# A state-space layer and a mixture of experts on one core: the ring of scan inputs, four slots or three

## The reference, cut to what matters

```python
h = x * rsqrt(mean(x * x) + EPS) * norm_scale
xs, res = split(h @ w_in, 2)
xs = silu(causal_depthwise_conv(xs, conv_w, conv_b)); res = silu(res)
delta, B, C = split(xs @ w_xproj, [dt_rank, dt_rank + N])      # N = 16 states
delta = softplus(delta @ w_dt + b_dt)
deltaA = exp(delta[..., None] * A)                             # A = -exp(A_log)
deltaBx = (delta * xs)[..., None] * B[:, :, None, :]
ys[t] = deltaA[t] * ys[t-1] + deltaBx[t]                       # the scan over time
y = einsum('blcn,bln->blc', ys, C)
x = layernorm(x + x + ((y + xs * D) * res) @ w_out)
```

## Time and profile before

| | before |
|---|---|
| time, median of 3 runs | 2160.95 us (2160.07 to 2165.15) |
| the profiled execution, its own time | 2160.5 us |
| its span | 2158.7 us |
| busy over the span: PE, DVE, ACT, POOL | 79%, 61%, 41%, 40% |
| mean granted clock of TensorE | 0.917 |

### The profile page before, as it was taken

The page is one execution under the profiler, slowest core; times in us unless marked ns, Lnnn a source line. Parts: engine busy times, 40 slices in busy tenths (PEclk is TensorE's granted clock), DMA queues, the critical chain, the costliest instruction groups (busy, mean ns, idle before and its releaser), DMA issues.

```text
span 2158.7 us, 20606 instructions
## 1 busy us (share of the span) xinstructions
PE 1710.6 (79%) x5491; PEld 821.9 (38%) x5492; DVE 1327.1 (61%) x1984; ACT 882.4 (41%) x1598; POOL 862.5 (40%) x399
## 2 busy tenths in 40 slices
PE   7387877878778787787765999949999999999900
PEld 2121312213122131221103767626666666676600
DVE  3379989798797987979994344413333333333345
ACT  4457556574565745657442333301221212212100
POOL 0766849577595775957850222210000000000065
PEclk9699989999899898998997999979999999999955
DMA  4633425334253342533416510010110101101033
GB/s 125 144 77 92 106 55 141 80 93 103 56 141 80 93 103 56 140 79 93 102 39 220 192 39 29 30 66 25 34 33 31 34 31 33 32 31 34 25 114 122
DMA packets 105433, 169.86 MB, mean 79 GB/s; under 512 B 14624, under 2 KB 53264, under 8 KB 105248
## 3 DMA queue, kind: packets, MB, share of 16 engines
q1 hardware_dynamic: 99232, 152.44, 27.3%
q0 software_dynamic: 6144, 16.79, 2.4%
HBM read 127.76 MB, written 41.42 MB: 78 GB/s over the span
## 4 chain that ended last, share of the span: by engine, by line
PE 52%; DVE 26%; ACT 8%; issue 7%; POOL 3%; DMA 3%; SPq 1%; another core or an unknown queue 0%; DVEq 0%; ACTq 0%; POOLq 0%
DVE psH L900 17%; PE psA L1382 12%; PE psP L1399 12%; DVE X L909 6%; PE psP L1228 5%; PE psP L1307 5%; PE psH L1316 5%; PE psA L1265 5%; PE psH L1390 3%; ACT psH L746 2%; PE psP L1217 2%; POOL gat L460 1%; PE psP L1236 1%; ACT L746 1%; DMA ud_dram<-ud 1%
## 5 line engine op out<-in xcount | busy, mean ns | idle before, releaser
L407 POOL TENSOR_TENSOR X<-rep,B 128x2048 f32<-128x2048 f32 x128 | 577.0, 4522 | 246.0 <-PE psA L1265 231.9
L1265 PE MATMUL psA<-X,gsum 128*32 128x512 f32 x1024 | 466.0, 677 | 238.7 <-DVE X L909 238.6
L746 ACT ACTIVATE psH<-rep,A_q 128x512 f32<-128x512 f32 x512 | 349.9, 689 | 123.6 <-DVE X L909 114.6
L900 DVE TENSOR_TENSOR_SCAN psH<-psH,X 128x512 f32<-128x512 f32 x256 | 313.0, 1223 | 119.6 <-ACT psH L746 75.6
L900 DVE TENSOR_TENSOR_SCAN psH<-psH,carry,X 128x512 f32<-128x512 f32 x256 | 329.8, 1288 | 48.0 <-ACT psH L746 48.0
L909 DVE TENSOR_TENSOR X<-psH,C 128x512 f32<-128x512 f32 x512 | 347.3, 679 | 0.0
L460 POOL DMA_INDIRECT gat<-eo_dram,slots x64 | 62.7, 980 | 664.9 <-DVE slots L1143 644.4
L1265 PEld LDWEIGHTS psA<-X,gsum 128*32 128x32 f32 x1024 | 59.7, 113 | 618.7 <-DVE X L909 575.9
L1382 PE MATMUL psA<-ew_s,nTb 128*128 x576 | 268.1, 608 | 0.8 <-ACT nTb L821 0.8
L1399 PE MATMUL psP<-ew_s,hT 128*128 x1152 | 262.2, 381 | 2.6 <-ACT hT L827 2.6
L1399 PEld LDWEIGHTS psP<-ew_s,hT 128*128 128x128 f32 x1152 | 220.0, 191 | 63.3 <-issue 36.8
(11 more groups left out here) (172 smaller groups left out, 1597.3 us busy)
## 6 DMA issues: line engine op xcount, KB each, us to landing
rep<-ud_dram SPq DMA_DIRECT2D x128, 512.0 KB, 8.7
ud_dram<-ud SPq DMA_DIRECT2D x32, 512.0 KB, 5.0
ew_s<-in_L_ffn_ew_dram SPq DMA_DIRECT2D x16, 1024.0 KB
xb<-rows_dram SPq DMA_DIRECT2D x72, 128.0 KB, 2.0
eo_dram<-eo SPq DMA_DIRECT2D x72, 128.0 KB, 1.7
B<-bc_dram SPq DMA_DIRECT2D x128, 64.0 KB, 2.3
C<-bc_dram SPq DMA_DIRECT2D x128, 64.0 KB, 2.1
out_dram<-fin SPq DMA_DIRECT2D x8, 512.0 KB
```

The source lines that it names most:

```text
L407: nc.gpsimd.tensor_tensor(X[:, Q % NX], rep[:, g % 2, 1], B4[:, f:f + 1, :].broadcast_to([P, NR, TC]), ALU.mult).then_inc(bx_ready, 1)
L746: nc.scalar.activation(psH[:, r, :], rep[:, g % 2, 0, r, :], ACT.Exp, scale=A_q[:, c, r, f:f + 1]).then_inc(dA_ready, 1)
L900: nc.vector.tensor_tensor_scan(psH[:, r, :], psH[:, r, :], X[:, Q % NX, r, :], start, ALU.mult, ALU.add).then_inc(scan_done, 1)
L1265: ins = nc.tensor.matmul(psA[r * GJ:(r + 1) * GJ, g % 2, :], gsum[:], X[:, Q % NX, r, :], start=False, stop=(f == NF - 1), skip_group_chec ...
```

## The change

The ring `X` has three slots instead of four. Nothing else is edited; the slot of step Q is `Q % NX` in the three places that use it (L407, L900 and L909, L1265), and POOL's wait at L406 is `y_acc >= Q - NX + 1`, so that it now waits for step Q - 3 where it waited for step Q - 4. The views of `X` that the start of the program uses (`vrows`, `st1`, `mv1`, `junk1`) lie in slots 0 to 2 and stay. `X` is the last tile of stage 1, so that no other tile moves; the 8 KB per partition stay unused.

```diff
         B4 = sb("B4", [P, NF, TC])
         C4 = sb("C4", [P, NF, TC])
-        NX = 4
+        NX = 3
         X = sb("X", [P, NX, NR, TC])
         vrows = X[:, 0, 0, 0:P]
         st1 = X[:, 1, 0, 0:NSUBS * 6].rearrange("p (t s) -> p t s", s=6)
```

## The result

| | before | after |
|---|---|---|
| time, median of 5 runs each | 2161.65 us (2160.07 to 2165.15) | 2175.09 us (2170.68 to 2177.53) |
| ratio, 95% interval | | 1.0052 (1.0040 to 1.0064) |
| profiled execution: span | 2158.7 us | 2173.3 us |
| end of the last scan in it | 1142.3 us | 1156.8 us |
| from there to the end | 1016.5 us | 1016.6 us |

The change costs half a per cent, and all of it in stage 1: behind the last scan the two profiles take the same time. The ratio in the table is taken from all the runs; the quotient of the two medians alone is 1.0062. The forecast was slower, 2171.3 us or a ratio of 1.0048, in a range of 2163.5 to 2174.5. Both ratios lie in that range, which is 1.0012 to 1.0063 of the 2160.95 us that it was set against. The median in us lies 0.6 us above it, 0.7 us of which come from the kernel before, whose median is 2161.65 with two more runs.

A forecast was written before the change was run, and what follows sets the result against it. DVE was the fullest engine, waiting mostly for ACT's exponential rather than POOL. Seven tile delays summed to 10.35 us, giving 2170.9 us profiled and 2171.3 us as median (ratio 1.0048), range 2163.5 to 2174.5.

The forecast's parts named there:

- What bounds: Stage 1: DVE, the fullest engine, waits for POOL only twice, 43.9 us, at the start; POOL waits for the ring.
- The chunk behind step 12: Tile 3, POOL: step 12 waits for PE's step 9, so chunk 0 of the next tile starts 2.28 us late.
- The transfers: SP's queue, tile 3: transfers land in issue order, so late loads of rep delay chunk 1's store and ACT 2.28 us.
- Is it given back?: DVE after step 14 of tile 3: no later wait found that recovers the 2.2 us, so the whole shift stays.
- The sum: Tiles 0 to 6: DVE delays of 0.35 to 2.25 us per tile add up to 10.35 us.
- the unknown: Where TensorE's lower clock falls: 5.6 us if PE's step 9 is quick everywhere, 11.3 if slow in tile 2 too.
- the clock after a longer wait: Unpriced piece, allowed 2 us together with ACT's first function on chunk 3, up to 2174.3 us.

The follow-up runs named there:

- e2: Four slots, every step of POOL but step 12 waiting for PE's step Q-3, against the kernel before; 2157.03 us against 2157.26, ratio 0.9999.
- e3: Three slots and four buffers of `ud` instead of two, against the kernel before; 2150.46 us, ratio 0.9964.
- e4: Three slots, store of chunk 1 directly behind the loads of rep, against the kernel before; 2155.20 us against 2157.26, ratio 0.9984.
- e8: Four slots, store of chunk 1 directly behind the loads of rep, against the kernel before; 2148.58 us against 2156.38, ratio 0.9963.
- e12: Three slots, four buffers of `ud`, store of chunk 1 directly behind the loads of rep, against the kernel before; 2152.25 us against 2156.77, ratio 0.9978.
- e10: Three slots, POOL's chunk 0 ahead of step 12, SP's step 0 loads of B behind rep's, against the kernel before; 2163.57 us against 2156.77, ratio 1.0028.

## Why the prediction was right

- *What bounds.* DVE does not wait for POOL in the changed kernel, though all but a few of POOL's steps are later: right, by the waits after and by e2.
- *The result as a number.* The direction and the place are right by mechanism. That the ratios 1.0048 and 1.0052 are so close is in part luck: in us the forecast was 3.8 too low, and the terms below were too small.
- *The chunk behind step 12.* Forecast 2.28 us late in tile 3; measured 586.3 - 583.7 = 2.6 us. The excess is the hand-over: PE's last product ends at 584.74 + 3.69 = 588.43 and POOL starts at 588.88, 0.45 us later where I took 0.1. In the other tiles it is 0.15. The excess did not reach ACT: the first store landed 2.6 us after its issue (598.57 to 601.17, the first load of rep), where it took 3.0 before, so the loads of rep were 2.2 us late and not 2.6. Two misses of some 0.4 us cancel here, which is luck.

```profile
584.74 3.69 PE L1265 MATMUL psA<-X,gsum 128*32 128x512 f32 x4 [1.26 <-DVE X L909]
```

- *The transfers.* Loads of C and the second store at their old places, the landing as late as the loads of rep: right, and shown by e3, e4 and e8 from three sides. That each transfer lands behind those issued before is too strong, though. It holds for every transfer of 512 KB in all profiles, and not for the loads of B and C, of 64 KB each: 12 of the 380 transfers of SP from 95 to 1130 us in the profile before landed ahead of an earlier one, all of them of B or C. The last load of rep issued at 997.61, and the load of B issued at 998.32, there:

```profile
DMA to landing us min/median/max: 11.9/11.9/11.9
...
DMA to landing us min/median/max: 10.0/10.0/10.0
```

997.61 + 11.9 = 1009.5 and 998.32 + 10.0 = 1008.3: the later one is there 1.2 us sooner, and 1.3 us is the most in any profile. The Trainium skill's sentence in "DMA: Bandwidth & Descriptors" ("Queues, rings and completion order"), by which completion is "not FIFO per issuing engine", agrees with these rows. The other half of that section, that each ring is worked off in order, agrees with the store of e4, 1.1 us behind the loads. The forecast hung on the large transfers alone, so its sum was not hurt.
- *Is it given back?* It was not: nothing in the split of after is negative, apart from single steps in which the clock's place differs.
- *The sum.* 10.35 us were forecast for the seven tiles; 11.3 and 11.8 were measured in the two profiles. By tile: 1.2, 2.1, 0.35, 2.25, 1.2, 2.05, 1.2 forecast, 1.3, 2.0, 1.3, 2.3, 1.3, 2.0, 1.1 measured. The term that was mis-sized is tile 2, where step 9 of PE did not have the quick products of the profile before (2.76 us). It was named as the unknown, and it went to the upper side, by its 0.9 us:

```profile
448.32 3.63 PE L1265 MATMUL psA<-X,gsum 128*32 128x512 f32 x4 [1.03 <-DVE X L909]
```

- *What was missing* is the rest of 3.2 us. Without it the median would not be past 2174.5. The term in the prediction is the 2 us for "the clock after a longer wait", in size too small and only as an allowance.
- *What is known of the rest.* It is 4.5 us more in step 3 of the tiles and 0.5 in step 4, less 1.2 in step 1 and 0.5 in step 8, where ACT waits for PE's projections and convolutions and DVE for ACT. TensorE's granted clock around the change from tile 3 to 4, steps 15 (first row) and 3 (second), in the kernel before and after:

```profile
613.90:621.00 7.10, 4.29 (x10) 0.55 (x8) 7.10 (x10) 5.85 (x11) 6.19 (x5) 1.00 0.12 39
645.00:653.40 8.40, 8.29 (x27) 3.06 (x28) 7.03 (x9) 4.52 (x12) 6.95 (x2) 1.00 0.23 64
...
623.20:630.30 7.10, 6.31 (x8) 0.68 (x8) 7.10 (x9) 5.86 (x11) 6.14 (x5) 0.57 0.16 39
654.30:664.40 10.10, 9.94 (x27) 3.41 (x30) 7.07 (x9) 4.57 (x12) 5.20 (x2) 0.83 0.22 57
```

(busy time and count of PE, PE's loads, DVE, ACT and POOL, then the mean granted clock, the share of the DMA engines and GB/s.) Behind the longer wait in step 14 the mean clock is 0.57 of full speed over step 15, and 0.83 over step 3, where it was 1.00 both times. Step 3 takes 10.1 us there and not 8.4. In the runs without the wait, e3 and e8, these steps gain 6 us instead, and their stretches of low clock are alike. That the rest goes with the place of the lower clock agrees with all of these. That the wait in step 14 is what moves it is not shown: e12, which has no such wait either, gained 2.8 us only, and e10 2.1. And e10 has the lower clock in a step 3 with no wait in step 14 before it. Step 15 of tile 0 and step 3 of tile 1, in the kernel before and in e10:

```profile
212.40:219.30 6.90, 4.18 (x8) 0.55 (x8) 6.89 (x9) 6.53 (x15) 5.75 (x5) 1.00 0.12 38
243.80:252.10 8.30, 8.18 (x24) 3.02 (x24) 7.29 (x10) 3.58 (x9) 6.85 (x2) 1.00 0.29 70
...
213.30:220.20 6.90, 4.21 (x10) 0.55 (x8) 6.90 (x9) 6.53 (x16) 6.74 (x6) 1.00 0.14 38
244.60:254.60 10.00, 9.84 (x24) 3.52 (x24) 7.33 (x10) 3.59 (x9) 5.04 (x2) 0.83 0.25 57
```

The same step takes 10.0 us and not 8.3 there. What moves the lower clock, and so the size of the rest, stays open.

## What to carry to other kernels

A ring's depth is not judged by whether its consumer waits for it. Follow every other piece in the producer's program: the slot bought idle time behind step 12, and the chunk that stood there was the head of a chain through a store, four loads and a queue, to a wait on another engine 24 us later (583.7 to 607.7 in tile 3). In the queue of this kernel a store landed when the large transfers before it had landed; its place in the line mattered more than its time of issue, so put what somebody waits for ahead of what nobody needs yet. Memory taken from a ring that is deep enough everywhere but once may be worth more elsewhere: the same 8 KB as two more buffers of `ud`, with three slots, is the kernel of e3, at 0.9964, and the order of e8 has the same gain (0.9963) without them.

## What the runs showed of the hardware

- Stores and loads of 512 KB in one queue landed in the order of issue in all 13 profiles, while single loads of 64 KB landed up to 1.3 us ahead of transfers issued before them. A store of 512 KB landed 2.6 us after its issue with nothing ahead of it (3.0 once, in the earlier trace rows), and 6.5 to 7.8 us in e4 and e8, issued directly behind four loads of 512 KB.
- Taking a wait away can come with more than its own length: in the profiles of e3 and e8 step 14 gave 2.9 us and the steps 1 to 8, whose work is the same, another 6; by the medians the two kernels gained 6.8 and 7.8 us in all. In e12 the steps 1 to 8 gave 2.8 us.
- Step 3 of tile 1, with the same 24 instructions of PE, took 8.3 us at a mean granted clock of 1.00 and 10.0 us at 0.83.
- The time from the last product of PE to POOL's start was 0.14 to 0.15 us in most places and 0.45 us in tile 3 of both profiles of the changed kernel. No run here tells why.
